# Twelve message-passing steps and two GCN layers: the sums of one destination tile by adding indirect transfers into two places

## The chip, the cores and the metric

The kernel runs on one core of one Trainium2 chip. The metric is the device time of one execution, in microseconds. The time before is the median of three runs; one further execution was profiled, and every row below is of that one.

## The reference, cut to what matters

```python
# x: 3125 x 128 (float32); src, dst: 53125 edges, sorted by dst, with one loop per node
h = maximum(layernorm(x), 0)
# first part: 12 steps
h = tanh(h @ W_in + b_in)
deg = clip(segment_sum(ones, dst), 1)
def step(h):
    agg = segment_sum(h[src], dst) / deg
    diff = tanh(gelu(agg @ W1 + b1) @ W2 + b2)
    return h + (diff - relu(clearance) * h) * 0.5
x = x + h_after_12_steps
# second part: layer norm, then two GCN layers with loops added and D^-1/2 (A+I) D^-1/2
h = maximum(layernorm(x), 0)
x = x + gcn(relu(gcn(h, G1, gb1)), G2, gb2)
```

## The kernel before

The sum over edges is a matrix product. In its entry phase the kernel builds the adjacency counts of all 3125 x 3125 node pairs in SBUF (`adj`, fp16, 25 source tiles of 128 rows by 3125 destination columns). It loads the edges, finds for each window of 5 destinations where its edges start (`here`, `chunk_d`, `start_i`), gathers 128 edges per window with five indirect transfers that GpSimd issues (L524), and turns them into one-hots on VectorE (`one_hots`, L1168), which TensorE multiplies, 12 windows a batch (`window`, L611), and ScalarE stores to `adj` (`evict`, L913). Between the batches the entry product of the network is placed: GpSimd applies the layer norm tile by tile (L530), TensorE transposes and multiplies, ScalarE applies Tanh. VectorE computes the degrees in its 4th batch, and in its 7th (`b == 6`) it compares the number of edges that were found with the number there is (`flag`). When edges are missing, every engine takes a general path, under `If(missed != 0)`.

Then come 12 steps. The state (`state`, fp32, 25 tiles) is split into two fp16 parts, `hi` (by ScalarE, L857) and `lo` (by VectorE, L1151). The destinations are seven groups: six of four tiles (512 columns, the one with the short tile 437), and group 6, `TAIL`, of tile 20 alone (128 columns). For each group of each step:

- TensorE: `edge_sums` (L715), for each of 25 source tiles hi rows times adjacency and lo rows times adjacency, 49 matmuls into one PSUM bank.
- VectorE: `means` (L1288), the sums times the inverse degree (`row`), into `agg`.
- TensorE: `hidden` (L748), two fp32 products with W1. ScalarE: `gelu` (L946), one Activate for each of the two halves.
- TensorE: `outputs` (L757), fp32 products with W2, two for each tile of 128 nodes (each stands in the trace as two passes). VectorE: `add_bias` (L1295). ScalarE: `tanh` (L955). VectorE: `update` (L1300), the new state.

The order on each engine is written out by hand and staggered. TensorE's `step` does, for g = 0 to 6, the sums of g, the outputs of g-2, the hidden products of g-1, and at the end the hidden products of group 6, the first eight source tiles of the next step's group 0, and the outputs of groups 5 and 6. ScalarE's `step` does, for g = 1 to 5, Tanh of g-2 and then Gelu of g-1; then it waits until the sums of all seven groups are done (`s_agg`), writes the next `hi` of groups 0 to 3, and goes on with Tanh of group 4 and Gelu of groups 5 and 6. VectorE's `step` does, for g = 0 to 5, the bias and update of g-2 and the means of g, then the means of group 6 and the next `lo`. The last step is another order on VectorE (`last_step`), which also adds the input, makes the second layer norm's factors and the loops. The first step sums with `first_sums`. SyncE and GpSimd do nothing in the steps; there is no traffic to DRAM in them. After the steps come two GCN layers with the same sums.

## Time and profile before

| what | before |
|---|---|
| median of 3 runs | 1300.9 us (1300.74 to 1300.9) |
| the profiled execution: its time | 1300.27 us |
| its span | 1298.5 us |
| TensorE matmuls busy | 1255.0 us (97%) |
| TensorE weight loads busy | 707.0 us (54%) |
| VectorE busy | 400.9 us (31%) |
| ScalarE busy | 298.3 us (23%) |
| GpSimd busy | 64.4 us (5%) |
| mean granted TensorE clock | 0.99 |
| moved by DMA | 13.77 MB, mean 11 GB/s |

Busy times overlap: weight loads run beside matmuls, and the engines beside each other. The share of busy time is a mean over the stages. Line numbers are those of the kernel before. A timeline row gives the start in us from the span's start, the duration of the row's instructions together in us, engine, line, operation, output <- inputs, count, and in brackets the idle time of the engine just before it and what ended it. A count of fp32 matmuls is one of passes.

### The profile page before, as it was taken

The numbers are of one execution on the slowest core, as the hardware profiler recorded it, in microseconds if no ns is written. First come the engines' busy times: TensorE is split into PE (matmuls) and PEld (weight loads), VectorE is DVE, ScalarE is ACT, GpSimd is POOL, SyncE is SP. The second block draws the span as 40 slices with busy tenths as digits, with TensorE's granted clock in tenths as the row PEclk, the third lists the DMA queues.
The fourth block names the chain that finished last, engine by engine and source line by source line (L and its number), as shares of the span: only waits on it lengthen the run. The fifth ranks groups of instructions, "written<-read, shape, count | busy, mean of one in ns | idle before, by whom it ended". The sixth has DMA issues, their size and how long they took to land.

```text
span 1298.5 us, 17275 instructions
## 1 busy us (share of the span) xinstructions
PE 1255.0 (97%) x7194; PEld 707.0 (54%) x7194; DVE 400.9 (31%) x817; ACT 298.3 (23%) x438; POOL 64.4 (5%) x56
## 2 busy tenths in 40 slices
PE   3888999999999999999999999999999999999998
PEld 1766465564565645645656456456564564565545
DVE  7999122131131221311312213113122132382312
ACT  1898221131121211311212113112121131120100
POOL 4940000000000000000000000000000000000000
PEclk7899999999999999999999999999999999999999
DMA  3000200000000000000000000000000000220101
GB/s 100 3 1 2 63 1 1 1 1 0 0 0 0 0 0 0 0 0 0 0 0 0 0 0 0 0 0 0 0 0 0 0 1 24 66 61 1 50 17 34
DMA packets 24552, 13.77 MB, mean 11 GB/s; under 512 B 6173, under 2 KB 23609, under 8 KB 24388
## 3 DMA queue, kind: packets, MB, share of 16 engines
q1 hardware_dynamic: 22334, 11.88, 3.4%
q10 hardware_dynamic: 1782, 1.06, 0.3%
q8 instruction: 26, 0.43, 0.1%
q0 software_dynamic: 400, 0.33, 0.1%
q14 instruction: 10, 0.08, 0.0%
HBM read 9.42 MB, written 3.44 MB: 10 GB/s over the span
## 4 chain that ended last, share of the span: by engine, by line
PE 88%; DVE 8%; issue 2%; DMA 1%; ACT 0%; DVEq 0%; SPq 0%; POOL 0%; ACTq 0%; POOLq 0%
PE ps L715 63%; PE ps L757 10%; PE ps L748 9%; DVE scratch L1168 5%; PE ps L628 3%; PE ps L829 1%; DVE lo L1151 1%; DMA adj<-packed_scratch,adj 1%; PE ps L611 0%; PE ps L571 0%; DVE cols L1367 0%; DMA adj<-in_dst_dram 0%; DVE state L1394 0%; PE ps L565 0%; DVE ps L1295 0%
## 5 line engine op out<-in xcount | busy, mean ns | idle before, releaser
L715 PE MATMUL ps<-adj,hi 128*128 128x512 f16 (+2 forms) x2275 | 747.2, 352 | 1.3 <-DVE lo L1151 1.3
L715 PE MATMUL ps<-adj,lo 128*128 128x512 f16 (+2 forms) x2184 | 730.4, 351 | 0.0
L715 PEld LDWEIGHTS ps<-adj,hi 128*128 128x128 f16 x2275 | 220.8, 97 | 228.0 <-issue 14.5
L715 PEld LDWEIGHTS ps<-adj,lo 128*128 128x128 f16 x2184 | 212.4, 97 | 224.1 <-issue 18.2
L1295 DVE TENSOR_TENSOR ps<-ps,bias 128x512 f32<-128x512 f32 (+1 forms) x84 | 53.9, 641 | 532.4 <-PE ps L757 532.4
L955 ACT ACTIVATE scratch<-ps 128x512 f32<-128x512 f32 (+1 forms) x84 | 46.3, 552 | 614.7 <-DVE ps L1295 614.6
L946 ACT ACTIVATE scratch<-ps,b1c,cols 128x512 f32<-128x512 f32 (+2 forms) x168 | 111.9, 724 | 170.7 <-PE ps L748 169.9
L757 PEld LDWEIGHTS ps<-w,scratch 128*128 128x128 f32 x1200 | 144.2, 192 | 8.1
L757 PE MATMUL ps<-w,scratch 128*128 128x128 f32 x1200 | 146.1, 275 | 0.0
L748 PE MATMUL ps<-scratch,w 128*128 128x512 f32 (+2 forms) x336 | 137.8, 538 | 0.0
L1288 DVE TENSOR_TENSOR scratch<-ps,scratch 128x512 f32<-128x512 f32 (+2 forms) x84 | 51.9, 619 | 178.7 <-PE ps L748 131.3
L1168 DVE TENSOR_TENSOR scratch<-scratch 128x1536 f16<-128x1536 f16 (+1 forms) x106 | 92.2, 940 | 0.5 <-PE ps L611 0.5
L913 ACT ACTIVATE adj<-ps 128x1500 f16<-128x1500 f32 (+1 forms) x52 | 76.0, 1480 | 14.9 <-PE ps L611 14.6
L748 PEld LDWEIGHTS ps<-scratch,w 128*128 128x128 f32 x336 | 57.3, 191 | 38.9 <-issue 37.2
L1300 DVE SCALAR_TENSOR_TENSOR state<-state,cols,scratch 128x512 f32<-128x512 f32 (+1 forms) x84 | 58.3, 694 | 47.0 <-ACT scratch L955 46.7
L611 PE MATMUL ps<-scratch 128*128 128x125 f16 x625 | 55.4, 249 | 13.2 <-DVE scratch L1168 11.9
L1151 DVE SCALAR_TENSOR_TENSOR lo<-state,cols,hi 128x512 f16<-128x512 f32 (+2 forms) x91 | 59.9, 672 | 13.6 <-ACT hi L857 12.8
L611 PEld LDWEIGHTS ps<-scratch 128*128 128x128 f16 x625 | 45.8, 110 | 29.0 <-DVE scratch L1168 25.7
L628 PE MATMUL ps<-adj,hi 128*128 128x512 f16 (+2 forms) x175 | 58.8, 353 | 1.6 <-ACT adj L933 1.6
L628 PE MATMUL ps<-adj,lo 128*128 128x512 f16 (+2 forms) x168 | 56.6, 352 | 0.0
L857 ACT ACTIVATE hi<-state,cols 128x512 f16<-128x512 f32 (+1 forms) x84 | 52.1, 669 | 19.4 <-PE ps L715 17.3
L530 POOL TENSOR_SCALAR state<-state,cols 128x128 f32<-128x128 f32 x25 | 49.2, 1981 | 11.4 <-DVE cols L1139 11.4
(143 smaller groups left out, 247.7 us busy)
## 6 DMA issues: line engine op xcount, KB each, us to landing
scratch<-rdeg_scratch SPq DMA_DIRECT2D x1, 1562.5 KB, 8.8
state<-in_x_dram SPq DMA_DIRECT2D x5, 256.0 KB, 3.7
scratch<-in_x_dram SPq DMA_DIRECT2D x5, 256.0 KB, 2.7
x_scratch<-state SPq DMA_DIRECT2D x5, 256.0 KB, 2.7
scratch<-dinv_scratch SPq DMA_DIRECT2D x5, 256.0 KB, 3.9
state<-x_scratch SPq DMA_DIRECT2D x5, 256.0 KB, 3.1
out_dram<-state SPq DMA_DIRECT2D x5, 256.0 KB
adj<-adj ACTq DMA_DIRECT2D x1, 390.6 KB, 9.1
```

The costliest lines, as they stand in the source:

```text
L611: return nc.tensor.matmul(target[:, :, place * WIN:(place + 1) * WIN], Lb[buf][:, b, :, i_], Rb[buf][:, b, :, i_].rearrange("p (k d) -> p ...
L628: mm = nc.tensor.matmul(ps[:, FIRST_BANK[g], 0:n], values[:, k, :], adj[:, k, c0:c0 + n], start=(at == 0 and values is hi), stop=(k == SHORT))
L715: return nc.tensor.matmul(bank, values[:, k, :], adj[:, k, c0:c0 + n], start=is_first, stop=is_last)
L748: nc.tensor.matmul(ps_hid_tail[h] if g == TAIL else ps_hid[h][:, 0:n], w1[:, h * FEAT:(h + 1) * FEAT], agg[g == TAIL][:, 0:n], start=True, ...
L757: mm = nc.tensor.matmul(ps_out[g == TAIL][:, i * FEAT:(i + 1) * FEAT], hid[g == TAIL][:, h, i * P:(i + 1) * P], w2[:, h, :], start=(h == 0 ...
L857: nc.scalar.activation(tiles_of(hi, group), tiles_of(state, group), ACT.Copy, scale=factor).then_inc(s_hi, 1)
L913: nc.scalar.activation(adj[:, :, bass.ds((i * 2 + u) * BATCH * WIN, BATCH * WIN)].rearrange("p k (b c) -> p b k c", b=BANKS), ps[:, 3 * u: ...
L946: nc.scalar.activation(hid[g == TAIL][:, h, 0:n], ps_hid_tail[h] if g == TAIL else ps_hid[h][:, 0:n], ACT.Gelu, bias=b1c[:, h:h + 1], scal ...
L1151: return V.scalar_tensor_tensor(out=lo[:, k0:k1, :], in0=values[:, k0:k1, :], scalar=0.0 if factor is None else factor, in1=hi[:, k0:k1, : ...
L1168: last_ = V.tensor_tensor(buf[:, 0:b, :, 0:w], c_.broadcast_to((128, b, m, w)), k_.broadcast_to((128, b, m, w)), ALU.is_equal)
L1295: V.tensor_tensor(p_, p_, bias_of(1, nt), ALU.add).then_inc(s_bias, 1)
L1300: V.scalar_tensor_tensor(out=tiles_of(state, g), in0=tiles_of(state, g), scalar=now_keep, in1=act_out[:, 0:n_], op0=ALU.mult, op1=ALU.add) ...
```

## The change

For the steps from the second to the last, the sums of group 6 (tile 20) no longer come from 49 matmuls. After each step SyncE stores the state to DRAM, row by row of a node (`state_dram`, with a zero row behind the last). GpSimd issues 32 indirect transfers of 128 rows: the c-th brings, for each of the tile's 128 destinations, the state row of its c-th edge's source (the zero row where there is none). The transfers alternate between two SBUF places (`tail_sum`, `PLACES = 2`); the first one on each place writes, the other 15 add. Each waits for the one before it on its place. TensorE then multiplies the two places with the identity into the bank, which adds and transposes them, and VectorE multiplies by the scale too (`now_tail`). The form with three places has 11, 11 and 10 transfers in a row; this one has 16 and 16.

On TensorE the hidden products of group 4 are issued ahead of the outputs of group 3. In the entry phase there is a sixth gather for the tile's edges (32 a row), with a sixth search for their starts, five small GpSimd operations that turn them into row numbers, and a check that every edge of the tile is among the 32 (`tail_degrees` on GpSimd after three layer-norm groups, a second product in `degree_total`, now after TensorE's 8th batch, and five small operations in VectorE's 9th batch, `b == 8`). ScalarE waits for the row numbers after its entry batches. VectorE's `update` waits for the store of the state before. Some small columns move to other places in SBUF. The general path keeps the matmuls. The core of the diff:

```diff
+CAP = 32
+PLACES = 2
+PLACE_TURNS = [len(range(i, CAP, PLACES)) for i in range(PLACES)]
...
+        state_dram = nc.dram_tensor("state_scratch", (NODES + 1, FEAT), F32).ap()
...
+        tail_sum = [w_in[:, :], bias[:, 0, :], hid[1][:, 0, :]][0:PLACES]
...
-        thresholds = place(WINDOWS)
-        past = place(WINDOWS)
-        here = place(WINDOWS)
+        thresholds = place(WINDOWS + P)
+        past = place(WINDOWS + P)
+        here = place(WINDOWS + P)
...
+            def store_state(t):
+                for g in range(NG):
+                    sp.wait_ge(s_upd, t * NG + g + 1)
+                    for sbuf, dram in rows(state, state_dram, g):
+                        sp.dma_start(dram, sbuf).then_inc(s_st[g], 16)
+
+            store_state(1)
+            with sp.Fori(2, STEPS) as t:
+                for i in range(PLACES):
+                    sp.wait_ge(s_place[i], t * (16 * PLACE_TURNS[i]) - 16 * PLACE_TURNS[i])
+                store_state(t)
...
+            pool.wait_ge(s_start, WCOLS + 1)
+            nc.gpsimd.indirect_dma_start(
+                tail_rows[:, :], None, packed_dram.rearrange("(n o) -> n o", o=1),
+                bass.IndirectOffsetOnAxis(ap=tail_start, axis=0)).then_inc(s_tedge, 16)
+            nc.gpsimd.memset(tail_block, 0.0)
+            pool.wait_ge(s_tedge, 16)
+            nc.gpsimd.tensor_scalar(tail_f, tail_rows[:, :], tail_base, None, ALU.subtract).then_inc(s_tc2, 1)
...
+            def tail_degrees():
+                pool.wait_ge(s_deg1, 1)
+                wg0, n0 = TAIL_WINDOWS
+                nc.gpsimd.affine_select(out=tail_block[0:WQ, 0:WIN], in_=deg[0:WQ, wg0 * WIN:(wg0 + 1) * WIN],
+                                        compare_op=ALU.is_ge, fill=0.0, base=-n0, pattern=[[1, WIN]],
+                                        channel_multiplier=WIN).then_inc(s_tc2, 1)
...
             for g, (k0, nt) in enumerate(GROUPS):
+                if g == 3:
+                    tail_degrees()
...
+            def gather_tail(t):
+                for g in range(NG):
+                    pool.wait_ge(s_st[g], t * (16 * parts(g)))
+                for c in range(CAP):
+                    i, turn = c % PLACES, c // PLACES
+                    before = (t - 1) * PLACE_TURNS[i] + turn
+                    if before:
+                        pool.wait_ge(s_place[i], 16 * before)
+                    nc.gpsimd.indirect_dma_start(
+                        tail_sum[i], None, state_dram, bass.IndirectOffsetOnAxis(ap=tail_rows[:, c:c + 1], axis=0),
+                        compute_op=ALU.bypass if turn == 0 else ALU.add).then_inc(s_place[i], 16)
...
             def degree_total():
                 pe.wait_ge(s_deg, 1)
-                nc.tensor.matmul(ps[0:1, 7, 64:65], deg_sum[0:WQ, :], ones_col[0:WQ, :], start=True, stop=True
-                                 ).then_inc(s_degsum, 1)
+                nc.tensor.matmul(ps[:, 7, 64:65], ones_col[0:WQ, :].broadcast_to((WQ, P)), deg_sum[0:WQ, :],
+                                 start=True, stop=True)
+                pe.wait_ge(s_tchk, 1)
+                nc.tensor.matmul(ps[:, 7, 96:96 + WIN + CAP], ones_col.broadcast_to((P, P)), tail_block,
+                                 start=True, stop=True).then_inc(s_degsum, 1)
...
-                if b == 4:
+                if b == 7:
                     degree_total()
...
+            def tail_sums(t):
+                bank = ps_agg[2][:, 0:P]
+
+                def place(i):
+                    pe.wait_ge(s_place[i], t * (16 * PLACE_TURNS[i]))
+                    return nc.tensor.matmul(bank, tail_sum[i], ident[:, :], start=(i == 0), stop=(i == PLACES - 1))
...
                         pe.wait_ge(s_aggT, t * NG + g - 1 + OPEN)
-                        edge_sums(t, g, (s_hi, s_lo), t * NG).then_inc(s_agg, 1)
+                        if g == TAIL:
+                            tail_sums(t).then_inc(s_agg, 1)
+                        else:
+                            edge_sums(t, g, (s_hi, s_lo), t * NG).then_inc(s_agg, 1)
+                    if g == TAIL - 1:
+                        hidden(t, g - 1)
                     if g >= 2:
                         outputs(t, g - 2)
-                    if g >= 1:
+                    if g >= 1 and g != TAIL - 1:
                         hidden(t, g - 1)
...
+            act.wait_ge(s_trow, 1)
+            act.wait_ge(s_norms_out, 32)
             with act.Fori(ENTRY_BATCHES // 2, BATCHES // 2) as i:
...
+                if b == 8:
                     dve.wait_ge(s_degsum, 1)
-                    link(V.tensor_copy(total[0:1, :], ps[0:1, 7, 64:65]))
-                    V.tensor_scalar(flag[0:1, 0:1], total[0:1, :], float(EDGES), None, ALU.not_equal).then_inc(s_flag, 1)
+                    V.tensor_scalar(total, ps[:, 7, 64:65], float(EDGES), None, ALU.not_equal)
+                    link(V.tensor_reduce(missing, ps[:, 7, 96:96 + WIN + CAP], AX.X, ALU.add))
+                    link(V.scalar_tensor_tensor(out=missing, in0=missing, scalar=0.0, in1=total, op0=ALU.not_equal,
+                                                op1=ALU.max))
+                    V.tensor_scalar(flag[0:1, 0:1], missing[0:1, :], 0.0, None, ALU.add).then_inc(s_flag, 1)
+                    V.tensor_scalar(missing_row, missing, float(NODES), None, ALU.mult).then_inc(s_mrow, 1)
...
+                if g == TAIL and not first:
+                    V.scalar_tensor_tensor(out=agg[1], in0=source[:, 0:n_], scalar=now_tail, in1=row[:, c0:c0 + n_],
+                                           op0=ALU.mult, op1=ALU.mult).then_inc(s_aggT, 1)
+                    return
...
             def update(t, g):
                 n_ = GROUPS[g][1] * FEAT
                 dve.wait_ge(s_tanh, t * NG + g + 1 + OPEN)
+                if not isinstance(t, int) or t > 0:
+                    dve.wait_ge(s_st[g], t * (16 * parts(g)))
```

## Rows read from the trace of the kernel before

**Rows 1.** The page: busy time of the engines, then the chain by line.

```profile
PE 1255.0 (97%) x7194; PEld 707.0 (54%) x7194; DVE 400.9 (31%) x817; ACT 298.3 (23%) x438; POOL 64.4 (5%) x56
...
PE ps L715 63%; PE ps L757 10%; PE ps L748 9%; DVE scratch L1168 5%; PE ps L628 3%; PE ps L829 1%; DVE lo L1151 1%; DMA adj<-packed_scratch,adj 1%; PE ps L611 0%; PE ps L571 0%; DVE cols L1367 0%; DMA adj<-in_dst_dram 0%; DVE state L1394 0%; PE ps L565 0%; DVE ps L1295 0%
```

**Rows 2.** Timeline, VectorE, one step apart; L715's sum over a step, clock last.

```profile
379.08 0.15 DVE L1311 TENSOR_SCALAR cols<-cols 128x1 f32 x1 [0.21 <-DVE lo L1151]
...
465.64 0.15 DVE L1311 TENSOR_SCALAR cols<-cols 128x1 f32 x1 [0.21 <-DVE lo L1151]
...
418.00:504.57 86.57, 66.00 (x345) 31.44 (x344) 1.00 0.00 0
```

**Rows 3.** Timeline, TensorE, the end of a step; the third row's matmul comes 49 times.

```profile
445.31 1.95 PE L757 MATMUL ps<-w,scratch 128*128 128x128 f32 x16
447.09 1.88 PE L748 MATMUL ps<-scratch,w 128*128 128x512 f32 x4
448.81 0.22 PE L715 MATMUL ps<-adj,hi 128*128 128x128 f16 x1
...
451.57 2.00 PE L757 MATMUL ps<-w,scratch 128*128 128x128 f32 x16
```

**Rows 4.** Timeline, VectorE, the same stretch.

```profile
447.29 0.70 DVE L1295 TENSOR_TENSOR ps<-ps,bias 128x512 f32<-128x512 f32 x1 [9.79 <-PE ps L757]
448.73 0.75 DVE L1300 SCALAR_TENSOR_TENSOR state<-state,cols,scratch 128x512 f32<-128x512 f32 x1 [0.74 <-ACT scratch L955]
449.40 0.61 DVE L1288 TENSOR_TENSOR scratch<-ps,scratch 128x437 f32<-128x437 f32 x1
...
463.52 0.35 DVE L1300 SCALAR_TENSOR_TENSOR state<-state,cols,scratch 128x128 f32<-128x128 f32 x1 [0.42 <-ACT scratch L955]
```

**Rows 5.** Timeline, ScalarE, the same stretch.

```profile
448.10 0.60 ACT L955 ACTIVATE scratch<-ps 128x512 f32<-128x512 f32 x1 [10.65 <-DVE ps L1295]
448.59 1.44 ACT L946 ACTIVATE scratch<-ps,b1c,cols 128x512 f32<-128x512 f32 x2
```

**Rows 6.** Timeline, VectorE and TensorE, the last step and the sums behind it.

```profile
1139.82 0.70 DVE L1295 TENSOR_TENSOR ps<-ps,bias 128x512 f32<-128x512 f32 x1 [1.17 <-PE ps L757]
...
1167.19 0.76 DVE L1151 SCALAR_TENSOR_TENSOR lo<-state,hi 128x384 f16<-128x384 f32 x2
...
1167.90 0.38 PE L715 MATMUL ps<-adj,hi 128*128 128x512 f16 x1 [0.34 <-DVE lo L1151]
```

**Rows 7.** Timeline at the indirect gathers, VectorE's index first; then the line's landings.

```profile
11.65 0.15 DVE L1080 TENSOR_SCALAR adj<-adj 125x1 int32<-125x1 f32 x1
...
12.84 1.41 POOL L524 DMA_INDIRECT adj<-packed_scratch,adj  x1 [2.67 <-issue]
14.55 1.21 POOL L524 DMA_INDIRECT adj<-packed_scratch,adj  x1 [0.31 <-issue]
...
DMA to landing us min/median/max: 3.1/3.4/3.6
```

**Rows 8.** DMA queue of GpSimd, 20.9 to 22.3 us: packets, MB, share of 16 engines.

```profile
q0 software_dynamic: 80, 0.07, 17.8%
```

**Rows 9.** DMA issues: a store of one tile's rows to DRAM, KB, us to landing.

```profile
x_scratch<-state SPq DMA_DIRECT2D x1, 64.0 KB, 1.6
```

**Rows 10.** Entry: engines' busy time in a window; timelines; layer-norm line L530.

```profile
50.00:100.00 50.00, 43.67 (x426) 33.07 (x427) 49.95 (x61) 46.66 (x46) 30.86 (x12) 1.00 0.05 2
...
48.96 1.01 PE L611 MATMUL ps<-scratch 128*128 128x125 f16 x12
...
49.60 0.77 DVE L1151 SCALAR_TENSOR_TENSOR lo<-state,cols,hi 128x512 f16<-128x512 f32 x1
...
31.68 49.18 POOL L530 TENSOR_SCALAR state<-state,cols 128x128 f32<-128x128 f32 x25 [11.38 <-DVE cols L1139]
...
L530 POOL TENSOR_SCALAR state<-state,cols x25: 443/2428/2696, 31.7 to 78.2; 128x128 f32<-128x128 f32 x25
...
31.68:47.16 15.48, 15.48 (x12) 0.69 0.01 1
```

More of the change, by code:

```diff
@@ L253, in gnn_kernel @@
         row_i = place(WINDOWS, talli)
+        tail_first, tail_base, tail_found, tail_start_f = (place(1, tall) for _ in range(4))
+        tail_start = place(1, talli)
+        tail_junk = place(CHUNK, tall)
         ones16 = place(1, tall).bitcast(F16)
@@ L337, in gnn_kernel @@
         g_degl = sem("general_degrees_loaded")
-        s_xr = [sem(f"x_reloaded{g}") for g in range(NG)]
         s_x2 = sem("x2_ready")
```

145 lines of the change are left out of this document (108 added, 37 removed).

## Prediction

> **What bounds the kernel now.** I read the page's busy times first, then its chain of work that ended last by line, then the timeline of one step for TensorE, VectorE and ScalarE, and last the few transfers that GpSimd issues. TensorE is busy for 97% of the span, and 63% of the chain lies in one line, the matmuls that add hi and lo rows into the sums over edges [rows 1]. The reader is to see that the eleven steps from the second on are a TensorE sequence with no holes. VectorE and ScalarE answer inside it, and most of their time is spent waiting for TensorE. A step takes 465.64 - 379.08 = 86.57 us, read from the first VectorE instruction of two steps in a row [rows 2].
>
> At the end of a step TensorE runs, in this order: the output products of group 3 (from 445.31), the hidden products of group 4 (447.09 to 448.81, so 1.72 us), the sums of the one-tile group 6 (448.81 to 451.57, so 2.76 us for 49 short matmuls), and the output products of group 4 at 451.57 [rows 3].
>
> **The part that is meant to go.** The change takes those 49 matmuls out of eleven steps (the first step keeps its own form) and puts two fp32 products with the identity in their place. One fp32 128x128 product stands in the trace as two passes, and the 16 passes of a group's output products take 447.09 - 445.31 = 1.78 us [rows 3], so four passes are 0.45 us. TensorE's own work falls by 2.76 - 0.45 = 2.3 us a step, 25 us in eleven.
>
> **What is late next.** I don't think that the 2.3 us come back. The output products of group 4 need both Gelu halves of group 4, and ScalarE runs Tanh of group 3 ahead of these. Tanh of group 3 needs VectorE's bias addition at 447.29, which starts 1.98 us after TensorE begins the output products of group 3 [rows 3, 4]. Tanh then runs at 448.10, and Gelu from 448.59 for 1.44 us, to 450.03 [rows 5]. Gelu thus ends 450.03 - 445.31 = 4.72 us after the output products of group 3 began, and today TensorE needs it 1.54 us later, because the 49 matmuls lie between. The change removes that cover, and it also swaps two calls: the hidden products of group 4 now go ahead of the output products of group 3. So these begin at 445.31 + 1.72 = 447.03, Gelu ends at 447.03 + 4.72 = 451.75, and TensorE starts the output products of group 4 at about 451.85 (0.1 us for the hand-over) where it started them at 451.57. A step becomes longer by 0.28 us, with 451.85 - 449.26 = 2.6 us of TensorE idle in it. The rest of the step follows as before: ScalarE's next hi rows wait for the last sums, which ended at 451.57, and Gelu frees ScalarE at 451.75, so they begin when they did. VectorE's state update of group 3 (448.73) and means of group 5 (449.40) move by 1.72 us [rows 4]. The means then end at about 451.7, and the hidden products of group 5 come 1.78 us after 451.85, so they are covered.
>
> In the last step VectorE has no idle time behind this point except a wait for the bias input of 1.17 us ahead of it [rows 6]. Its row of work after that wait moves by the full 1.72 us, the lo rows of group 5 (1167.19) with it, and TensorE already waits 0.34 us for these [rows 6]. This step costs 1.72 us. The steps together: 10 x 0.28 + 1.72 = 4.5 us.
>
> **The transfers that do the sum now.** After every step SyncE stores the seven groups of the state (8 transfers), and GpSimd then issues 32 indirect transfers of 128 rows x 512 B, alternating between two places. Each one waits until the one before it on its place has landed. A place is thus a chain of 16 links of length T, and T is not in the trace. The nearest rows are the five plain indirect gathers of the same shape (125 rows x 512 B) [rows 7]. From issue to landing they take 3.1 to 3.6 us. What lies between the release and the issue shows in two forms: 0.31 us behind another gather, and 12.84 - 11.80 = 1.04 us where GpSimd had stood idle and VectorE's index (11.65 + 0.15) came last. The addition isn't in any row. The last gathers moved 80 packets, 0.07 MB, in 17.8% of 1.4 us on 16 engines [rows 8], so 0.25 us of engine time; a second read of the same size adds 0.25 us or nothing. If the read of the destination needs descriptors of its own, it adds up to one more 1.21 us of issue [rows 7]; if not, nothing. T lies between 3.1 + 0.3 = 3.4 and 3.6 + 1.04 + 0.25 + 1.21 = 6.1 us. I take 1.04 + 3.1 + 0.6 = 4.74 us: the issues wait one by one, as the first gather did, and 0.6 is half of what a second set of descriptors would cost.
>
> The fixed part of the cycle: from the end of the group's sums (451.57) to the end of the last state update (463.52 + 0.35 = 463.87) 12.3 us [rows 3, 4], the store of group 6 landing 1.6 us after its issue [rows 9], 0.45 us of products, and the second place starting 1.21 + 0.31 = 1.52 us behind the first [rows 7]. Together 15.9 us, so the cycle is 16T + 15.9. It has to fit into 86.57 + 0.28 = 86.85 us, and it does up to T = 4.43 us. With T = 4.74 it is 91.7 us, 5.2 us more than today's step. Eleven gathers give 11 x 5.2 = 57 us, in which the 4.5 us above are contained. Behind the waiting product on TensorE are queued the output products of group 4, the hidden products and the next step's sums; ScalarE's next hi rows wait for it too. Behind the waiting GpSimd instruction stands nothing but its own gathers. SyncE's next stores wait for the places, but only from the moment the sums are done, and the last group's store comes 12 us later anyway. TensorE's granted clock is 1.00 over the step, its 2.4 GHz level [rows 2]; I assume that holes of 3 to 8 us don't change that. If they did, the 66 us of sums in a step would grow; no row of a step shows by how much.
>
> The Trainium skill (DMA: Bandwidth & Descriptors, Anatomy of one DMA — SWDGE (gpsimd) path) gives a transfer issued on GpSimd 2.0 us plus its bytes at 436 GB/s, an estimate of 2.15 us for 64 KB. By it T would be 3.2 us with the release, the cycle 67 us, and the transfers would be hidden: the first rival. The trace disagrees, with 3.1 to 3.6 us.
>
> **The entry.** GpSimd gets one more gather and five small operations ahead of its layer-norm rows. These start at 31.68, after an 11.4 us wait for VectorE's factors [rows 10], and a gather of 3.1 us with some 2 us of small operations fits in that. VectorE's extra 1 us for the sixth start falls into its wait for the gathers. The larger one-hots of the chunks (753 columns for 625) add 0.3 us at the start, estimated from their share of two operations under 0.9 us. The check moves from the 7th to the 9th batch on VectorE, and TensorE does its part after its 8th, which began at 48.96 and takes 1.0 us. With the shift and four fp32 passes the result is there at about 50.9. VectorE needs five small operations of 0.15 to 0.2 us (as the one at 379.08 [rows 2]), so it goes on at 51.7 where it was free at 49.6. It is busy 49.95 of 50 us in this stretch [rows 10], so the delay stays: 2.1 us, less the 0.3 us of the old check, plus 0.3 us at the start, 2.1 us in all. GpSimd's part of the check comes after 12 layer-norm tiles, which are done at 47.16 [rows 10], nearly 4 us ahead of 50.9; its two small selections take a tile's time at most, 2.7 us each [rows 10]. In the worst case they cost 1.7 us more. I bound the entry's term by 0 and 6 us.
>
> **The sum.** The profiled execution took 1300.27 us (span 1298.5 and 1.8 around it); the median of the three runs is 1300.9. 1300.3 + 57 + 2.1 = 1359.4, say 1360 us.
>
> **Rivals.**
> (a) *The gathers are hidden*, T below 4.43 us. For it: the landing itself is 3.1 us, and with a release of 0.31 us there is 1 us to spare for the addition. Against it: the only issue after an idle wait took 1.04 us. The time is 1300.3 + 4.5 + 2.1 = 1306.9 us, slower by 0.5%; with an entry that costs nothing it is 1304.8, with a cheap hand-over 1302.
> (b) *Gelu of group 4 is not what TensorE waits for*, so that the 2.3 us come back in each step. That needs Tanh of group 3 to be off the path; the place is ScalarE's queue between 448.10 and 450.03 and it decides as soon as the bias of group 3 is ready 1.8 us earlier than I place it. Then 1300.3 - 25 + 2.1 = 1277 us, the faster side. Only if T is below 4.3 us as well. Against it stand the rows of each step.
> (c) *The general path is taken*, because a row of this tile has more than 32 edges. The program would then be many times slower. The mean is 17 edges a row and the seeded inputs reach 26 in this tile, so 1 in 100.
>
> **How the numbers follow.** Exposed gathers 0.55 (1360, own range 1312 to 1450, which is T from 4.45 to 5.2; at 5.2 the cycle is 99.1 us, 11 x 12.5 + 2 = 140 us more). Hidden gathers 0.35 (1302 to 1312). Gain back 0.08. General path and longer links 0.02. The range holds the first two and leaves the gain out: 1303 to 1450. What this kernel's measurement can tell from no change is about 0.2%, 2.6 us. Faster than that takes (b), 0.08. Within it takes (a) with a free entry, 0.09. Slower 0.83.
>
> **What would show it.** In the profile after: TensorE's sums line loses 11 x 49 matmuls; the output products of group 4 start 2.6 us or more after the identity products (hidden) or right behind products that wait for a transfer (exposed); the bias addition of group 3 is 1.7 us later relative to the end of group 5's sums; the distance of two indirect issues on one place is T, and the step is 16T + 15.9 where T is over 4.43. GpSimd's last landing before the sums comes early if (a) holds. The prediction is wrong if the step is under 86.5 us, if T is under 4.4, or if VectorE isn't held at its 9th batch.

## The result and the profile after

| kernel | median us | lowest to highest | kernel before beside it | ratio, 95% interval |
|---|---|---|---|---|
| after | 1323.39 | 1320.63 to 1328.43 | 1300.9 | 1.0177 [1.0146, 1.0208] |

The changed kernel is slower by 1.8%, where 1360 us, 4.6%, was forecast. The direction was right, the size and its cause were not. That 1323 us lies among the times that I gave for exposed gathers (1312 to 1450) is luck: the gathers are hidden, and something else costs the time. Of the nine runs of the kernel before that stood beside e4, e5, e7 and e8, one took 2220.92 us at a mean granted clock of 0.557 and is left out below. The profiled execution took 1320.63 us (before: 1300.27), with a span of 1319.0 us (1298.5), and the mean granted clock of TensorE is 0.979 (0.990). The DMA engines moved 54.55 MB for 13.77 MB.

The page of the kernel after: busy time of the engines, then the chain that ended last, by line. Both stand against [rows 1].

```profile
PE 1248.5 (95%) x6703; PEld 696.0 (53%) x6703; DVE 404.7 (31%) x839; ACT 298.5 (23%) x438; POOL 598.9 (45%) x420
...
PE ps L816 60%; PE ps L877 11%; PE ps L868 10%; DVE scratch L1301 4%; PE ps L729 3%; PE ps L954 1%; DVE ps L1439 1%; PE ps L712 1%; ACT scratch L1073 1%; DVE lo L1284 1%; DMA adj<-packed_scratch,adj 1%; PE ps L669 0%; DVE cols L1516 0%; DMA adj<-in_dst_dram 0%; PE ps L663 0%
```

491 records of matmuls are gone, but TensorE is busy for only 6.5 us less, although 25 us of its work were taken out. And in the chain there is no indirect transfer: TensorE never waits for one in the full steps. In the last step it waits 0.65 us for one, and with three places, without that wait, the last step and what follows take the same time (228.67 and 228.66 us). So the 57 us that I forecast for waits on gathers aren't there, and something makes the rest of TensorE's work dearer.

The timeline of the kernel after, VectorE, at the same instruction near the start of three steps in a row (L1460 is L1311 of before), then the windows of the steps between them: length, busy time and count of TensorE, its weight loads, VectorE, ScalarE, GpSimd, then granted clock, DMA share and GB/s.

```profile
472.62 0.15 DVE L1460 TENSOR_SCALAR cols<-cols 128x1 f32 x1
...
561.16 0.15 DVE L1460 TENSOR_SCALAR cols<-cols 128x1 f32 x1
...
648.01 0.15 DVE L1460 TENSOR_SCALAR cols<-cols 128x1 f32 x1
...
472.62:561.16 88.54, 86.15 (x428) 46.45 (x427) 18.49 (x35) 16.85 (x28) 48.80 (x32) 0.98 0.26 42
561.16:648.01 86.85, 84.46 (x428) 45.41 (x427) 18.42 (x34) 16.63 (x28) 49.36 (x32) 1.00 0.27 43
```

Two steps of the same work, 88.54 and 86.85 us against 86.57 before [rows 2]. The second is the forecast without exposed gathers, to the hundredth. TensorE is idle for 2.39 us in either (length less busy time); the first differs in the granted clock, and so in how long the same work keeps TensorE busy. From the first step's start to the last one's there are eleven steps. The first takes 65.17 us (before 64.92), the second 87.02 (86.64), the one at 561.16 takes 86.85, and the other eight 88.35 to 88.54.

The end of one of the long steps, TensorE first, then VectorE and ScalarE, then a window behind it. It answers to [rows 3 to 5].

```profile
538.63 1.88 PE L868 MATMUL ps<-scratch,w 128*128 128x512 f32 x4
540.35 1.95 PE L877 MATMUL ps<-w,scratch 128*128 128x128 f32 x16
542.13 0.39 PE L847 MATMUL ps<-ident,w_in 128*128 128x128 f32 x2
542.36 0.39 PE L847 MATMUL ps<-ident,bias 128*128 128x128 f32 x2
545.13 2.56 PE L877 MATMUL ps<-w,scratch 128*128 128x128 f32 x16 [2.39 <-ACT scratch L1073]
...
542.33 0.70 DVE L1439 TENSOR_TENSOR ps<-ps,bias 128x512 f32<-128x512 f32 x1 [11.44 <-PE ps L877]
...
543.15 0.60 ACT L1082 ACTIVATE scratch<-ps 128x512 f32<-128x512 f32 x1 [12.37 <-DVE ps L1439]
543.64 1.44 ACT L1073 ACTIVATE scratch<-ps,b1c,cols 128x512 f32<-128x512 f32 x2
...
546.51:549.92 3.41, 3.41 (x11) 2.23 (x10) 2.17 (x4) 2.33 (x4) 0.00 (x0) 0.50 0.00 0
```

The identity products don't wait. The output products of group 4 do, 2.39 us (this idle time of TensorE is called the hole from here on), for the Gelu halves of group 4, and these end 543.64 + 1.44 - 540.35 = 4.73 us after the output products of group 3 began (4.72 in [rows 3, 5]). 1.4 us after the hole, at 546.51, the granted clock goes to 0.50 (1.2 GHz) for 3.41 us, with TensorE busy for all of them. It costs 88.5 - 86.85 = 1.65 us of the step, which is what half the speed over 3.41 us makes (1.7). In the kernel before no step shows such a fall.

The ten holes from the second step on are of the same length, but the fall doesn't stand at one distance behind them. Here is the hole that follows the step without a fall, and the window of its fall:

```profile
720.52 3.68 PE L877 MATMUL ps<-w,scratch 128*128 128x128 f32 x16 [2.39 <-ACT scratch L1073]
...
720.59:724.00 3.41, 3.41 (x16) 3.41 (x17) 0.86 (x2) 2.32 (x4) 0.00 (x0) 0.50 0.28 77
```

In order of the steps: the first hole has no fall; then the fall begins 0.92, 1.16 and 1.38 us after the hole's end; then comes the hole without one (it ends at 633.67); then 0.07, 0.34, 0.60, 0.84 and 1.08 us. Falls in neighbouring steps start 88.75 us apart (457.77 and 546.51), the steps with a fall are 88.5 us long, and so the fall comes some 0.25 us later behind the hole in each step, until one is left out. The length of the hole alone thus doesn't decide; its place in time does too.

The 20.4 us of the profiled executions are therefore: the entry 2.45 (first step at 143.40 us for 140.95), the steps 16.4, of which 8 falls x 1.65 = 13.2 and the longer steps 3.2, and the last step with what follows it 1.6.

### The profile page after: what moved, and what is told of

The parts are those of the page before. It is cut to its first block, busy times and chain, and to the rows that moved or that the text cites. A ratio compares the mean times of both kernels' runs of the same rounds, so it can differ in the third digit from the quotient of the medians.

```text
span 1319.0 us, 17027 instructions
## 1 busy us (share of the span) xinstructions
PE 1248.5 (95%) x6703; PEld 696.0 (53%) x6703; DVE 404.7 (31%) x839; ACT 298.5 (23%) x438; POOL 598.9 (45%) x420
## 2 busy tenths in 40 slices
DMA packets 108438, 54.55 MB, mean 41 GB/s; under 512 B 13068, under 2 KB 107135, under 8 KB 108266
## 4 chain that ended last, share of the span: by engine, by line
PE 86%; DVE 8%; issue 3%; ACT 1%; DMA 1%; DVEq 0%; ACTq 0%; SPq 0%; POOL 0%; POOLq 0%
PE ps L816 60%; PE ps L877 11%; PE ps L868 10%; DVE scratch L1301 4%; PE ps L729 3%; PE ps L954 1%; DVE ps L1439 1%; PE ps L712 1%; ACT scratch L1073 1%; DVE lo L1284 1%; DMA adj<-packed_scratch,adj 1%; PE ps L669 0%; DVE cols L1516 0%; DMA adj<-in_dst_dram 0%; PE ps L663 0%
## 5 line engine op out<-in xcount | busy, mean ns | idle before, releaser
L816 PE MATMUL ps<-adj,hi 128*128 128x512 f16 (+2 forms) x2000 | 715.7, 370 | 2.0 <-DVE lo L1284 2.0
L816 PE MATMUL ps<-adj,lo 128*128 128x512 f16 (+2 forms) x1920 | 698.8, 370 | 0.0
L626 POOL DMA_INDIRECT w_in<-state_scratch,tail_rows x176 | 268.6, 1526 | 467.9 <-DMA state_scratch<-state 384.2
L816 PEld LDWEIGHTS ps<-adj,hi 128*128 128x128 f16 x2000 | 194.6, 97 | 226.1 <-issue 12.6
L626 POOL DMA_INDIRECT bias<-state_scratch,tail_rows x176 | 269.0, 1529 | 77.8 <-DMA bias<-state_scratch,tail_rows 55.6
L816 PEld LDWEIGHTS ps<-adj,lo 128*128 128x128 f16 x1920 | 186.6, 97 | 220.4 <-issue 14.6
L877 PE MATMUL ps<-w,scratch 128*128 128x128 f32 x1200 | 155.0, 285 | 25.9 <-ACT scratch L1073 25.9
L877 PEld LDWEIGHTS ps<-w,scratch 128*128 128x128 f32 x1200 | 151.6, 200 | 40.7 <-ACT scratch L1073 28.5
L868 PE MATMUL ps<-scratch,w 128*128 128x512 f32 (+2 forms) x336 | 143.1, 555 | 0.0
L868 PEld LDWEIGHTS ps<-scratch,w 128*128 128x128 f32 x336 | 61.3, 201 | 42.9 <-issue 39.7
L729 PE MATMUL ps<-adj,hi 128*128 128x512 f16 (+2 forms) x175 | 58.8, 353 | 1.6 <-ACT adj L1060 1.6
L729 PE MATMUL ps<-adj,lo 128*128 128x512 f16 (+2 forms) x168 | 56.6, 352 | 0.0
```

The source lines that it names most:

```text
L626: nc.gpsimd.indirect_dma_start(tail_sum[i], None, state_dram, bass.IndirectOffsetOnAxis(ap=tail_rows[:, c:c + 1], axis=0), compute_op=ALU. ...
L729: mm = nc.tensor.matmul(ps[:, FIRST_BANK[g], 0:n], values[:, k, :], adj[:, k, c0:c0 + n], start=(at == 0 and values is hi), stop=(k == SHORT))
L816: return nc.tensor.matmul(bank, values[:, k, :], adj[:, k, c0:c0 + n], start=is_first, stop=is_last)
L868: nc.tensor.matmul(ps_hid_tail[h] if g == TAIL else ps_hid[h][:, 0:n], w1[:, h * FEAT:(h + 1) * FEAT], agg[g == TAIL][:, 0:n], start=True, ...
L877: mm = nc.tensor.matmul(ps_out[g == TAIL][:, i * FEAT:(i + 1) * FEAT], hid[g == TAIL][:, h, i * P:(i + 1) * P], w2[:, h, :], start=(h == 0 ...
```

## Experiments

Every kernel ran beside the kernel before on its own chip. Medians in us; "before" is that of the same chip. e4, e8 and e9 ran once each.

| label | edit | median | before | ratio, 95% interval |
|---|---|---|---|---|
| e1_outputs_first | swap of the two calls undone | 1293.92 | 1301.06 | 0.9944 [0.9927, 0.996] |
| e2_filled_hole | 22 matmuls in the hole | 1308.74 | 1301.06 | 1.0063 [1.0046, 1.008] |
| e3_three_places | three places | 1321.64 | 1301.06 | 1.0158 [1.0141, 1.0175] |
| e4_one_place | one place | 1938.52 | 1301.87 | one run |
| e5_before_swapped | before, with the swap alone | 1305.56 | 1301.87 | 1.003 [1.0017, 1.0043] |
| e6_no_transfers | before, short tile's sums gone, no gathers | 1320.34 | 1301.06 | 1.0151 [1.0134, 1.0168] |
| e7_three_first_late | e1, three places, look in the 10th batch | 1287.59 | 1301.87 | 0.9891 [0.9873, 0.9908] |
| e8_spread_zero_rows | a zero row for each partition | 1320.67 | 1301.87 | one run |
| e9_all_zero_row | every index is the zero row | 1363.46 | 1301.79 | one run |
| e10_three_first | e1, three places | 1289.12 | 1301.79 | 0.9906 [0.9888, 0.9924] |

### Is it the hole? The hole filled

Theory: the hole of 2.4 us in TensorE's work makes the clock fall. Rival: the transfers, or their traffic, make it fall or stretch the step.

```diff
+                    if g == TAIL and not last:
+                        for _ in range(22):
+                            nc.tensor.matmul(ps[:, 7, 256:512], adj[:, 10, 256:384], adj[:, 10, 0:256],
+                                             start=True, stop=True)
```

> The changed kernel with 22 matmuls of 256 columns on TensorE, 2.35 us of work whose result nobody reads, in the hole after the two identity products in the ten loop steps with a successor. They finish before Gelu of group 4, so nothing waits for them. Theory A (the granted clock falls because of the hole): no fall of the clock in these steps, every step 86.85 us, the kernel 13 us faster than the changed one, about 1308 us. Rival B (transfers or GpSimd cause it): steps stay at 88.5 us and the kernel at 1321 us or above.

Measured 1308.74 us, ratio 1.0063 [1.0046, 1.008]. TensorE's timeline at the end of a step of this kernel (L894 is the filling), and the window over ten steps, for this kernel and then for the kernel after.

```profile
539.39 0.39 PE L847 MATMUL ps<-ident,w_in 128*128 128x128 f32 x2
539.62 0.39 PE L847 MATMUL ps<-ident,bias 128*128 128x128 f32 x2
539.84 2.57 PE L894 MATMUL ps<-adj 128*128 128x256 f16 x22
542.39 2.05 PE L877 MATMUL ps<-w,scratch 128*128 128x128 f32 x16
...
200.00:1070.00 870.00, 870.00 (x4490) 475.70 (x4489) 186.38 (x334) 168.98 (x286) 489.32 (x320) 1.00 0.26 43
```

```profile
200.00:1070.00 870.00, 848.48 (x4212) 457.49 (x4211) 178.92 (x322) 161.82 (x272) 488.45 (x320) 0.99 0.26 41
```

TensorE does 2.57 us more work in ten steps, and the kernel is 14.7 us faster by the medians (12.6 by the spans). The output products of group 4 start right behind the filling, which is 542.39 - 539.39 = 3.00 us behind the first identity product, as in the kernel after (545.13 - 542.13 = 3.00). The ten full steps are 86.7 to 87.0 us and the granted clock stays at 1.00 in them. The transfers are all there. Empty or filled, the place takes the same 3.00 us; it is the fall of the clock behind the empty one that costs 13 us.

### Is it the transfers? The same hole without them

The kernel before, with the swap of the two calls and this edit; it leaves out the sums of tile 20.

```diff
+                        if g == TAIL:
+                            bank = ps_agg[2][:, 0:P]
+                            nc.tensor.matmul(bank, w_in[:, :], ident[:, :], start=True, stop=False)
+                            nc.tensor.matmul(bank, bias[:, 1, :], ident[:, :], start=False, stop=True).then_inc(s_agg, 1)
+                        else:
+                            edge_sums(t, g, (s_hi, s_lo), t * NG).then_inc(s_agg, 1)
```

> The kernel before, with the 49 matmuls of group 6 in the eleven later steps replaced by two identity products of constant tiles and with the swap on TensorE; no stores of the state, no gathers, no change of the entry. It leaves out the sums of tile 20. Theory A: the hole and the falls of the granted clock come from the order of work alone, so the steps take 88.5 us where the clock falls and 86.85 where it does not, and the kernel about 1317 us. Rival B (transfers needed for the fall): steps of 86.85 us, the kernel 1305 us.

Measured 1320.34 us, 1.0151 [1.0134, 1.0168]. TensorE's timeline in this kernel (L757 is the output products), a window behind the hole, and the one over ten steps.

```profile
540.38 0.39 PE L770 MATMUL ps<-ident,w_in 128*128 128x128 f32 x2
540.60 0.39 PE L771 MATMUL ps<-ident,bias 128*128 128x128 f32 x2
543.38 2.91 PE L757 MATMUL ps<-w,scratch 128*128 128x128 f32 x16 [2.39 <-ACT scratch L953]
...
544.37:547.78 3.41, 3.41 (x13) 2.62 (x12) 1.79 (x4) 1.99 (x4) 0.00 (x0) 0.50 0.00 0
200.00:1070.00 870.00, 848.48 (x4220) 458.30 (x4219) 175.96 (x311) 159.97 (x268) 0.00 (x0) 0.99 0.00 0
```

DMA share and GpSimd are at nothing, and yet the hole of 2.39 us, the fall for 3.41 us, the steps of 88.5 us and TensorE's 848.48 us are those of the kernel after; the falls come in eight of the ten full steps here too. So neither the gathers nor their 40 GB/s are needed for the loss. The spans differ by 1.8 us (1317.2 and 1319.0), and the first step starts 1.4 us earlier without the gathers' preparation.

### Which part of the change makes the hole?

e5 makes this edit in the kernel before, e1 undoes it in the kernel after.

```diff
+                    if g == TAIL - 1:
+                        hidden(t, g - 1)
                     if g >= 2:
                         outputs(t, g - 2)
-                    if g >= 1:
+                    if g >= 1 and g != TAIL - 1:
                         hidden(t, g - 1)
```

> The kernel before with only the swap on TensorE, the hidden products of group 4 ahead of the outputs of group 3; the 49 matmuls stay. Theory A: Gelu of group 4 ends at 451.75 where TensorE needed it at 451.57, so TensorE waits some 0.3 us a step, the granted clock stays 1.00, steps of 86.85 us and 1.7 us more in the last step: 4.5 us more than before, 1305.5 us. Rival B (the swap is free while the 49 matmuls stand behind it): 1301 us.

> The changed kernel with the swap on TensorE undone: outputs of group 3 go ahead of the hidden products of group 4 again. Theory A (the hole ahead of the outputs of group 4 costs by itself and by the granted clock): Gelu of group 4 ends 1.72 us earlier, the hole shrinks from 2.4 us to about 0.85 us, the granted clock stays 1.00 through the steps, a step takes 85.1 us, and the kernel about 1289 us, 12 us faster than before. Rival B (the transfers are what TensorE ends up waiting for, or their traffic slows it): the step stays at 88.5 us and the kernel at 1320 us, or it falls by no more than 1 us a step because the last gather now lands late.

The swap alone: 1305.56 us, 1.003 [1.0017, 1.0043], and the span goes from 1298.5 to 1303.0, the 4.5 us of the forecast's term. By parts it is less exact: 2.4 us lie in the steps, 1.7 in the last step and what follows, and 0.35 in the entry, which the swap doesn't touch. Its full steps are 86.85 us, and no step has a fall of the clock: the 49 short matmuls still fill the place, so the swap costs 0.28 us a step.

The swap undone: 1293.92 us, 0.9944 [0.9927, 0.996]. This is the first kernel of the study that beats the one before. TensorE at the end of a step, VectorE at the same instruction near the start of this step and the next, and TensorE over ten steps:

```profile
530.95 1.95 PE L877 MATMUL ps<-w,scratch 128*128 128x128 f32 x16
532.74 1.88 PE L868 MATMUL ps<-scratch,w 128*128 128x512 f32 x4
...
534.67 0.39 PE L847 MATMUL ps<-ident,bias 128*128 128x128 f32 x2
535.73 2.05 PE L877 MATMUL ps<-w,scratch 128*128 128x128 f32 x16 [0.67 <-ACT scratch L1071]
...
464.94 0.15 DVE L1458 TENSOR_SCALAR cols<-cols 128x1 f32 x1
...
550.08 0.15 DVE L1458 TENSOR_SCALAR cols<-cols 128x1 f32 x1
...
200.00:1070.00 870.00, 863.27 (x4359) 464.09 (x4358) 191.79 (x347) 170.79 (x290) 494.99 (x325) 1.00 0.27 44
```

With the output products of group 3 first, Gelu of group 4 starts 1.72 us sooner, the hole is 0.67 us, the clock stays at 1.00, and a step is 85.13 us, 1.44 less than before. So 1.44 of the 2.3 us of TensorE's work do come back once the swap is gone; 0.67 us of hole keeps most of the rest. The swap cost the change twice: 1.72 us in each of these steps by the place of Gelu, and 1.65 us more in eight of the ten by the clock.

The same kernel shows where two places are short. TensorE in its last step, then a window:

```profile
1131.77 0.46 PE L847 MATMUL ps<-ident,w_in 128*128 128x128 f32 x2 [1.22 <-DMA w_in<-state_scratch,tail_rows]
1134.38 0.80 PE L847 MATMUL ps<-ident,bias 128*128 128x128 f32 x2 [2.16 <-DMA bias<-state_scratch,tail_rows]
...
1133.69:1140.52 6.83, 6.14 (x21) 5.01 (x22) 3.49 (x11) 2.64 (x5) 0.00 (x0) 0.50 0.44 109
```

Here the gathers land late by 1.22 and 2.16 us, and the clock falls for 6.83 us; the last step and what follows takes 230.86 us, for 226.9 in the two kernels with three places below.

### How long is a link? One place, three places

This is e4; e3 has a 3 there.

```diff
-PLACES = 2
+PLACES = 1
```

> The changed kernel with one place: a chain of 32 gathers in each of eleven steps. Here the chain must show, so it tests the formula of the forecast, step = links x T + fixed part, with a T that two places hide. From the changed kernel's rows: landings of 3.3 to 4.2 us plus 0.3 us of release give T = 4.0 us, the fixed part from the last landing to the next first issue is 16.7 us, so a step of 145 us and a kernel of about 1950 us. If a release takes the 1.04 us that the forecast had, T is 4.8 us, the step 170 us and the kernel 2220 us.

> The changed kernel with three places in place of two, so chains of 11, 11 and 10 transfers and one more identity product of 0.23 us that falls into the hole. Theory A: the transfers were hidden, so the time does not move (within 3 us of the changed kernel, 1321 to 1328 us), while the 32 gathers are issued every 1.85 us and end some 5 us earlier in a step. Rival B (two places are too few): the step falls towards 85 us and the kernel to 1290 us or less.

One place takes 1938.52 us. The timeline of this kernel: GpSimd's last gather of a step and the next step's first, TensorE's first product behind them, and two windows (a whole cycle; the part in which TensorE waits).

```profile
763.93 1.55 POOL L626 DMA_INDIRECT w_in<-state_scratch,tail_rows  x1 [2.88 <-DMA w_in<-state_scratch,tail_rows]
785.97 0.99 POOL L626 DMA_INDIRECT w_in<-state_scratch,tail_rows  x1 [20.50 <-DMA state_scratch<-state]
...
768.11 0.79 PE L847 MATMUL ps<-ident,w_in 128*128 128x128 f32 x2 [58.27 <-DMA w_in<-state_scratch,tail_rows]
...
642.05:785.97 143.92, 85.65 (x426) 46.60 (x425) 18.51 (x33) 16.74 (x28) 48.93 (x32) 0.80 0.16 26
713.09:771.12 58.03, 3.01 (x14) 3.01 (x15) 1.10 (x2) 2.18 (x4) 18.56 (x12) 0.50 0.16 25
```

The first gather of the step is issued at 642.05 and the 32nd has landed at 768.07: 126.0 / 32 = 3.94 us a link. From there to the next first issue are 17.9 us, which is the fixed part for one place. The cycle is 143.9 us. The expectation, 145 us a step and 1950 us in all, was worked out from a link of 4.0 us and a fixed part of 16.7 us in the rows of the kernel after, and it is borne out. Exposed gathers look like this; in the full steps of the kernel after there are none. TensorE waits from 709.84 to 768.11. The clock falls 3.3 us after the wait begins and stays at 0.50 for 58.03 us, until 3.0 us after it ends.

With three places the time is 1321.64 us, and its interval [1.0141, 1.0175] overlaps that of the kernel after: the third place brings nothing there, since TensorE waits for Gelu and not for the second place. The third identity product shortens the hole to 2.17 us; the clock falls in eight of the ten full steps all the same, and they are 88.5 us.

The gathers of the kernel after in one step, GpSimd's timeline: the first five issues and the last four. Then the page's row of their issues, with the median us from issue to landing, and the landings of all gathers by the view of L626.

```profile
474.46 1.00 POOL L626 DMA_INDIRECT w_in<-state_scratch,tail_rows  x1 [25.29 <-DMA state_scratch<-state]
475.76 0.96 POOL L626 DMA_INDIRECT bias<-state_scratch,tail_rows  x1 [0.30 <-issue]
477.42 1.57 POOL L626 DMA_INDIRECT w_in<-state_scratch,tail_rows  x1 [0.69 <-DMA w_in<-state_scratch,tail_rows]
479.29 1.55 POOL L626 DMA_INDIRECT bias<-state_scratch,tail_rows  x1 [0.30 <-issue]
481.14 1.54 POOL L626 DMA_INDIRECT w_in<-state_scratch,tail_rows  x1 [0.30 <-issue]
...
529.57 1.55 POOL L626 DMA_INDIRECT w_in<-state_scratch,tail_rows  x1 [0.63 <-DMA w_in<-state_scratch,tail_rows]
531.79 1.55 POOL L626 DMA_INDIRECT bias<-state_scratch,tail_rows  x1 [0.67 <-DMA bias<-state_scratch,tail_rows]
534.05 1.55 POOL L626 DMA_INDIRECT w_in<-state_scratch,tail_rows  x1 [0.72 <-DMA w_in<-state_scratch,tail_rows]
536.22 1.55 POOL L626 DMA_INDIRECT bias<-state_scratch,tail_rows  x1 [0.62 <-DMA bias<-state_scratch,tail_rows]
...
w_in<-state_scratch,tail_rows POOLq DMA_INDIRECT x176, 3.7
...
DMA to landing us min/median/max: 2.5/3.7/5.1
```

Landings are counted from the start of the issue. The first two write and don't add: 1.00 and 0.96 us of issue, landing after 2.6 us (2.5 to 2.7 in the full steps). Each adding one takes 1.55 us of issue with 0.30 us between two, so a place comes round every 2 x 1.85 = 3.70 us even if nothing is waited for: at first GpSimd's issuing sets the pace, not the landing (3.2 to 3.3 us from issue). Late in the step the landing has grown to 4.15 us, and the link, the distance on one place, is 534.05 - 529.57 = 4.48 us. (The 5.1 us stands in the last step, where loads and stores for what follows run beside the gathers.) All 32 together take 65.9 us, from 474.46 to the last landing at 540.37, and have ended 1.8 us before the product at 542.13. The wait on a landing ends 0.3 us after it.

### Why the landing grows from 3.2 to 4.2 us

The rows of this tile have 17 edges on average; where a row has no more edges, its index points to the one row of zeros. In late gathers most partitions thus read the same 512 B. Theory: this makes the landing longer. Rival: it's the load of the sums beside it, or the queue filling up.

The edit of e8 stands above the dots, that of e9 below them.

```diff
-("state_scratch", (NODES + 1, FEAT), F32)
+("state_scratch", (NODES + P, FEAT), F32)
+            nc.gpsimd.iota(zero_row, pattern=[[0, 1]], base=NODES, channel_multiplier=1, **big)
-            nc.gpsimd.tensor_scalar(tail_f, tail_f, float(NODES), None, ALU.min)
+            nc.gpsimd.tensor_scalar(tail_f, tail_f, zero_row, None, ALU.min)
...
-            nc.gpsimd.tensor_scalar(tail_rows[:, :], tail_f, missing_row, None, ALU.max)
+            nc.gpsimd.tensor_scalar(tail_rows[:, :], tail_f, 0.0, float(NODES), ALU.mult, ALU.add)
```

> The changed kernel with 128 zero rows in DRAM, one for each partition, in place of one; the number of transfers and bytes is the same. Theory A (the landings grow from 3.3 to 4.2 us over the 32 because ever more partitions read the same row): every landing 3.2 to 3.5 us, the last issue of a step some 6 us earlier, time unchanged (1320 to 1325 us). Rival B (they grow for another reason, such as VectorE's work or the number in the chain): 4.2 us at the end as before.

> The changed kernel with every row number of the 32 gathers set to that of the zero row, so that all 128 partitions read the same 512 B in each. It leaves out the sums of tile 20 (they are zero). If landings grow with the share of partitions that read one row, every gather from the third on takes 4.2 us to land, a place's link 4.45 us, the chain 71 us in place of 66, and the last gather lands some 5 us later in the step, which the hole nearly covers: steps of 88.5 us or up to 3 us more. If the growth came from the place in the chain, the early gathers land in 3.3 us as before.

The page's row of DMA issues, first of e8, then of e9; the row of the kernel after, 3.7 us, stands above.

```profile
w_in<-state_scratch,tail_rows POOLq DMA_INDIRECT x176, 3.2
```

```profile
w_in<-state_scratch,tail_rows POOLq DMA_INDIRECT x176, 4.2
...
578.00:670.00 92.00, 87.60 (x429) 47.84 (x427) 18.52 (x33) 16.97 (x28) 48.41 (x32) 0.96 0.26 40
```

With 128 zero rows, one for each partition, the adding gathers of this step land after 3.1 to 3.4 us up to the last, the place comes round in 3.71 us to the end, and the last gather of a step lands some 6 us sooner (534.42 for 540.37). With all partitions on one row the adding ones land after some 4.2 us from the start of the chain on (median; 3.5 to 3.9 us for the first, which only writes), all 32 take 72.4 to 73.3 us in the full steps, and now they are exposed: steps of 90.4 to 92.2 us, 1363.46 us in all. Number, size and order of the transfers are the same in the three kernels, so it is the one row. In the kernel after this is hidden, and e8, with 1320.67 us, is within the spread of the kernel after. One run each is enough for the landings, which repeat in every step, but not for a difference in time of a microsecond.

### Both faults away

e10 has the first two parts of this edit in the kernel after, e7 all three.

```diff
-PLACES = 2
+PLACES = 3
-                    if g == TAIL - 1:
-                        hidden(t, g - 1)
                     if g >= 2:
                         outputs(t, g - 2)
-                    if g >= 1 and g != TAIL - 1:
+                    if g >= 1:
                         hidden(t, g - 1)
...
-                if b == 8:
+                if b == 9:
                     dve.wait_ge(s_degsum, 1)
```

> The outputs of group 3 first and three places, with the look at the edge count in VectorE's 9th batch as in the changed kernel. The run with the later look reached the steps 3 us late as well, so: theory A (the later look brought nothing, because TensorE fell to its 1.2 GHz level there) 1287 to 1290 us, the same as with the later look; rival B (the later look was worth its 1.4 us) 1289.5 us or more and the steps beginning later by that.

> The outputs of group 3 first again, three places, and VectorE's look at the edge count one batch later (10th for 9th). Theory A: the steps take 85.1 us as with two places, the last step loses its wait for the last gather, which cost 2.2 us with two places and the outputs first, and VectorE's wait of 1.4 us at the entry goes; together 3 to 4 us less than with the outputs first alone, about 1290 us. Rival B: the entry is held elsewhere and the last step by something other than the gathers, 1294 us.

Outputs first and three places: 1289.12 us, 0.9906 [0.9888, 0.9924]. Against e1 the steps are the same (85.14 us), and the last step and what follows are 226.9 us for 230.86, the 3.9 us that its late gathers took there. Moving VectorE's look at the edge count to the 10th batch as well: 1287.59 us, 0.9891 [0.9873, 0.9908]. The intervals overlap; with the look later, the start of the first step (145.34 us) and the first step itself (63.5) add up to 208.8 us, for 208.1 in e10, so nothing is shown for it. Both beat the kernel before by about 1%, and the changed kernel by 2.7 to 2.8% (0.9906 and 0.9891 for 1.0177).

## Why the prediction was right and wrong

**Right: what is late next.** Gelu of group 4 ends the hole, 4.73 us after the output products of group 3 begin (4.72 forecast). The hole is 2.39 us (2.6), the step without a fall of the clock 86.85 us (86.85), the last part of the program 1.6 us longer (1.72). With the swap alone the span grows by 4.5 us (4.5), where the last tenths are luck, as the parts above show. Taking 2.3 us a step from TensorE brought nothing, as said.

**Wrong: the likeliest case.** I gave 0.55 to gathers that TensorE waits for, 57 us of them, and they are hidden. The step that failed is the size of the link: I took T = 1.04 + 3.1 + 0.6 = 4.74 us, and it is 4.0. The release of 1.04 us was read at a gather that had waited for VectorE's index after a long idle time [rows 7]; it is 0.87 us at the first gather of a step too, behind 25 us of idling (landing at 562.16, issue at 563.03), but inside the chain it is 0.3 us, like the 0.31 that I had as the lower bound. The landing of an adding gather is 3.2 to 3.3 us where I had 3.1 + 0.6 = 3.7. Against the writing gathers of the same step (2.6 us) the addition does cost 0.6 to 0.7 us, 0.55 of it issue (1.55 for 1.00); what was too big was the landing of 3.1 us that I added it to. With two places GpSimd's issuing is a bound of its own, 2 x 1.85 = 3.70 us a link, which I had not counted. What I had not named either, the common zero row, adds up to 1 us in late gathers. In all a link is 3.94 us with one place and (540.37 - 475.76) / 16 = 4.0 us with two, inside my bounds of 3.4 to 6.1 but under the turning point of 4.43. Of the three signs of being wrong that I named, this one came. The form of the sum, links times T and a fixed part, held in the test with one place (145 us expected, 143.9 measured); the size of T didn't. The ends that I gave for exposed gathers don't follow from that form either: T = 4.45 gives 1308 us and T = 5.2 gives 1440, where I wrote 1312 and 1450. Nothing hangs on it.

**Mis-sized: the fixed part.** From the last landing to the next first issue I had 12.3 + 1.6 + 0.45 and a release of 1.04, 15.4 us; one place shows 17.9. One missing term is the last store. In the step above it was issued at 559.28 and landed at 562.16, 2.9 us later and not 1.6 [rows 9]. It was issued 1.0 us behind a store of 192 KB on its queue; the one of the row stood 3.3 us behind such a store. I take this for the cause; it wasn't tested apart. The other, in the kernel with one place, is the clock: after the long wait TensorE runs at 0.50 for three more microseconds (until 771.12), so the identity products and the output products take 0.59 and 2.95 us between starts for 0.45 and 1.78, 1.3 us more. How near the kernel after is to the turning point can be read directly: its last gather lands 1.8 us before the product, and a product up to 2.4 us later would still be ahead of Gelu. So by this estimate a link could grow by (1.8 + 2.4) / 16 = 0.26 us from 4.0, to about 4.3 and not to 4.43.

**Wrong: the assumption on the clock.** I assumed that holes of 3 to 8 us leave the granted clock at 1.00, and gave it no price. A hole of 2.4 us already costs 1.65 us in eight steps of ten that have it. Had I stayed with rival (a), 1306.9 us, this term of 13.2 us would have been all that was missing: 1320.1, for 1320.63 in the profiled execution. With the hole filled, (a) is nearly what is measured: 1308.07 in the profiled execution, 1308.74 as the median.

**The entry.** 2.1 us forecast, 2.45 in the profiled execution. VectorE, in the kernel after:

```profile
51.58 0.16 DVE L1324 TENSOR_SCALAR cols<-ps 128x1 f32<-128x1 f32 x1 [1.39 <-PE ps L678]
...
53.11 7.14 DVE L1301 TENSOR_TENSOR scratch<-scratch 128x1536 f16<-128x1536 f16 x8
```

It waits 1.39 us for the count and runs its small operations until the next batch at 53.11. GpSimd's two selections for it started at 49.36 and 50.31 and were ready at 50.5, and TensorE's product began at 51.15. I had called them covered by nearly 4 us; that step was wrong, though the sum differs by a third of a microsecond only. Among the kernels with this entry the first step starts at 143.3 to 145.6 us, so the term itself isn't known to better than 2 us, and that it came out so near is luck.

**Rival (b)** was rightly held off as long as the swap was there. It would be decided, I wrote, by a bias of group 3 that is ready 1.8 us earlier. With the swap undone it is ready 1.72 us earlier, and then 1.44 us a step come back and not 2.3: 1293.92 us and, with three places, 1289.12, not 1277.

## What to carry to other kernels

Before you take work from the engine that sets the time, ask what that work covered, and order the calls around the gap so that the longest chain through the other engines starts first: here the order of two calls is worth 2.3% once the work is gone (1.0177 for 0.9944), and 0.3% while it is there. Price a hole by the granted clock behind it too, not by its length alone; here 2.39 us of hole cost 1.65 us more in most steps. For a chain of indirect transfers, find out which of the two sets its pace, landing or issue. Where the landing does, spread the padding indices over several rows: here that shortened the chain by 6 us, which was worth nothing only because the chain was hidden.

## What the runs showed of the hardware

**A short hole lowers TensorE's clock.** 2.39 us idle in a stream that is busy all the time otherwise is followed, 0.07 to 1.38 us later, by 3.41 us at 1.2 GHz, in eight of the ten steps that have such a hole. The kernels with the same hole and no transfers (e6), with a hole of 2.17 us (e3) and with spread zero rows (e8) show eight of ten as well. In all four the fall comes 0.2 to 0.3 us later behind the hole from one step to the next, up to 1.4 us, then one step has none, and then it begins again at 0.1 us. So which holes get a fall goes with their place in time; what sets that isn't shown by these runs. With 0.67 us idle in every step (e1), 0.45 us (e7 and e10) or none (e2) no full step had one; between 0.67 and 2.17 us nothing was tried. In the last steps, 0.85 and 1.19 us idle close together were followed by a fall in e2, 0.65 and 1.40 us in the kernel after by none, and 1.22 and 2.16 us in e1 by one of 6.83 us. Where TensorE waited for 58.3 us (e4), it was at 1.2 GHz for 58.03 us, from 3.3 us after the wait's start to 3.0 us after its end.

**Adding indirect gathers on GpSimd** (128 rows of 512 B): issue 1.55 us, and 0.96 to 1.00 for one that only writes; landing 3.2 to 3.3 us after the start of the issue, and 2.5 to 2.7 for one that only writes; a wait on a landing ends 0.3 us after it. The Trainium skill (DMA: Bandwidth & Descriptors, Anatomy of one DMA — SWDGE (gpsimd) path) makes it 2.15 us for 64 KB, by the estimate from its figures; the traces show more, by 0.35 us or more for the writing and over 1 us for the adding ones.

**One row read by most partitions is slow.** An adding gather lands after 4.2 us (median) when all 128 partitions read the same 512 B of DRAM (e9), and after 3.2 us when each partition without an edge has a zero row of its own (e8), in transfers that are otherwise the same.
